# Attention values computed query by query: probabilities stationary, attention split by token and then turned

## The reference, cut to what matters

```python
def _L0_attn_ref(x, W_attn, b_attn, W_proj, b_proj):      # x: (2, 2048, 256), 16 heads of 16
    qkv = x @ W_attn + b_attn
    q, k, v = split(qkv)                                   # heads: (b, 16, t, 16)
    scores = einsum('bhtd,bhsd->bhts', q, k) * 0.25
    mask = (j <= i) & (j >= i - 64)                        # local, causal
    attn = softmax(where(mask, scores, -inf))
    out = einsum('bhts,bhsd->bhtd', attn, v)               # the step that the change rewrites
    return out.reshape(b, t, c) @ W_proj + b_proj

x = layernorm(x + attention(x))
# then a routed FFN: argmax router over 8 experts, W1[e] (256 x 1024), gelu, shared Wo
x = layernorm(x + ffn(x))
```

## Time and profile before

| what | value |
|---|---|
| median of 3 runs | 600.46 us (595.09 to 601.87) |
| the profiled execution, its own time | 598.72 us |
| span of its trace | 597.0 us |
| mean granted clock of TensorE | 0.957 |
| PE / DVE / ACT / POOL busy | 518.8 / 430.5 / 364.2 / 333.5 us |
| first instruction stretch, attention loop, tables, FFN | about 0 to 44, 44 to 352, 352 to 365, 365 to 597 us |

### The profile page before, as it was taken

One profiled execution on the slowest core, in us unless ns is written; L12 is line 12 of the kernel. 1 busy time (PEld: TensorE's weight loads), 2 busy tenths in 40 slices (PEclk: granted clock), 3 DMA queues, 4 the chain that ended last, 5 costly groups with the idle time before them and its releaser, 6 DMA issues. The chain is left out here.

```text
span 597.0 us, 29744 instructions
## 1 busy us (share of the span) xinstructions
PE 518.8 (87%) x11019; PEld 445.0 (75%) x11019; DVE 430.5 (72%) x1137; ACT 364.2 (61%) x832; POOL 333.5 (56%) x579
## 2 busy tenths in 40 slices
PE   4689896999999999989887716999999999999990
PEld 3577684877787777777775505999999999998870
DVE  4437784888788777877876665688888888886543
ACT  3436673787775757666674723766677676675450
POOL 7821442455553446444554541588888888886433
PEclk9869997999999999999999966999999999999996
DMA  9696987586757776566745102133322222221100
GB/s 202 152 213 175 244 237 201 157 189 182 200 164 210 172 202 178 164 183 187 191 140 152 38 27 68 52 100 97 94 83 73 66 81 74 74 73 49 31 9 7
DMA packets 94908, 77.46 MB, mean 130 GB/s; under 512 B 37030, under 2 KB 88367, under 8 KB 94770
## 3 DMA queue, kind: packets, MB, share of 16 engines
q1 hardware_dynamic: 91410, 67.12, 43.4%
q0 software_dynamic: 3264, 8.41, 4.0%
q10 hardware_dynamic: 96, 0.04, 0.0%
HBM read 43.63 MB, written 23.62 MB: 113 GB/s over the span
## 5 line engine op out<-in xcount | busy, mean ns | idle before, releaser
L1447 PE MATMUL ps<-v_even,w_hi 128*128 128x128 f16 (+1 forms) x1280 | 170.5, 215 | 1.7 <-issue 0.7
L1447 PE MATMUL ps<-v_even,w_lo 128*128 128x128 f16 (+1 forms) x640 | 132.1, 214 | 0.2
L853 ACT ACTIVATE probs<-ps,b1T 128x128 f32<-128x128 f32 (+1 forms) x320 | 87.3, 361 | 72.1 <-PE ps L1447 60.4
L1429 PE MATMUL ps<-wo_hi,ks 128*128 128x256 f16 x576 | 128.6, 273 | 1.0 <-DVE ks L1113 1.0
L1447 PEld LDWEIGHTS ps<-v_even,w_hi 128*128 x1280 | 120.8, 98 | 6.4 <-issue 3.1
L892 DVE TENSOR_REDUCE mx<-ps 128x4 bf16<-128x512 f32 x128 | 84.5, 683 | 18.9 <-PE ps L1219 18.0
L1429 PE MATMUL ps<-wo_lo,ks 128*128 128x256 f16 x288 | 78.5, 272 | 0.0
L1271 PE MATMUL ps<-probs,sel 128*32 128x64 f32 x2048 | 67.0, 220 | 6.4 <-issue 6.4
L745 ACT ACTIVATE probs<-ps 128x512 f32<-128x512 f32 x128 | 69.5, 617 | 2.7 <-PE ps L1245 2.6
L1113 DVE TENSOR_TENSOR ks<-probs,ks 128x512 f16<-128x512 f32 x72 | 55.1, 765 | 19.4 <-ACT ks L860 19.2
L1447 PEld LDWEIGHTS ps<-v_even,w_lo 128*128 x640 | 62.7, 98 | 6.2 <-issue 0.5
(11 more groups left out here) (232 smaller groups left out, 1360.1 us busy)
## 6 DMA issues: line engine op xcount, KB each, us to landing
qk_s<-qk_hi SPq DMA_DIRECT2D x64, 128.0 KB
w_in<-in_L_ffn_W_dram SPq DMA_DIRECT2D x32, 256.0 KB, 4.5
v_odd<-slots SPq DMA_DIRECT2D x64, 128.0 KB, 2.1
qs<-qk_s SPq DMA_DIRECT2D x16, 384.0 KB, 4.4
ks<-qk_s SPq DMA_DIRECT2D x16, 384.0 KB, 5.3
v_even<-v_odd SPq DMA_DIRECT2D x63, 96.0 KB, 4.0
ks<-qk_s SPq DMA_DIRECT2D x32, 144.0 KB, 4.0
qk_s<-qk_lo SPq DMA_DIRECT2D x32, 128.0 KB
```

Of the source, the lines that this page charges most:

```text
L853: last = nc.scalar.activation(g[1 - p][:, ic, n * width:(n + 1) * width], ps_h[1 - p][:, half, col + n * width:col + (n + 1) * width], ACT ...
L1429: ins = mm(ps_y[p], h[p][hs][:, ic, :], wo[ws][:, ic, :], start=n == 0, stop=n == 3 * IC - 1)
L1447: up_ins = mm(ps_h[1 - p][:, half, col + m * width:col + (m + 1) * width], weights(ws, owners[m], k, ic), sT[1 - p][ss][:, k, at], start=k ...
```

## The change

The value matmuls are turned round. For each head and each block of 64 queries the probabilities (128 keys x 64 queries) are the stationary operand and v of that head moves, 16 columns and a 17th that holds W_UP = 64 and so gives the denominator. The result (`ps_num`) has queries on the partitions, 16 heads x 17 columns. `sel`, `spread`, `less` and their set-up are gone. DVE takes the reciprocal of 128 x 16 denominators and multiplies at once (`att`, tokens x 256 channels), both now ahead of bn_stats. POOL splits `att` as before. PE then turns the two f16 parts with four transposes, which stand behind all four pieces of queries and keys and wait for POOL's `al_done`; ACT copies the result (`attT`, 512 f16 columns) where it copied rdenT. The projection of old moves from behind the x transposes to directly behind scores(0). values(0) and values(1) now take a half of the heads each; values(0) stands behind the x transposes and waits for three of the four exponentials, values(1) behind scores(3).

```diff
-    VW = 3 * HD
+    VW = HD + 1
...
-        v_odd = [sb(f"v_odd{k}", [P, PAIRS, VW], f32) for k in range(VRING)]
-        v_even = [sb(f"v_even{k}", [P, PAIRS, VW], f32) for k in range(VRING)]
+        v_odd = [sb(f"v_odd{k}", [P, HEADS, VW], f32) for k in range(VRING)]
+        v_even = [sb(f"v_even{k}", [P, HEADS, VW], f32) for k in range(VRING)]
...
+        rden = sb("rden", [P, HEADS], f32)
+        att = sb("att", [P, C], f32)
+        att_part = [sb(f"att_{s}", [P, C], f16) for s in ("hi", "lo")]
+        attT = sb("attT", [P, 2, CC, P], f16)
...
+        ps_num = ps[:, 6, 0:HEADS * VW].rearrange("p (h w) -> p h w", h=HEADS)
+        ps_attT = ps[:, 7, 0:C].bitcast(f16).rearrange("p (s k t) -> p s k t", s=2, k=CC)
...
+            link(nc.gpsimd.tensor_copy(ident_h[:, :], ident[:, :]))
...
-            link(nc.gpsimd.memset(sel[:, :, :], DEN))
...
-            link(nc.gpsimd.memset(spread[:, :, :], 0.0))
...
             for k in range(VRING):
-                nc.gpsimd.memset(v_odd[k][:, :, :], 0.0)
+                nc.gpsimd.memset(v_odd[k][:, :, :], W_UP)
...
                     pool.wait_ge(att_done, n + 1)
-                    wait(pool, proj_done, n)
-                    nc.gpsimd.tensor_copy(attT[0][:, :, :], att[:, :, :]).then_inc(ah_done, 1)
+                    wait(pool, attT_done, n)
+                    nc.gpsimd.tensor_copy(att_part[0][:, :], att[:, :]).then_inc(ah_done, 1)
                     pool.wait_ge(ah_done, n + 1)
-                    nc.gpsimd.tensor_tensor(attT[1][:, :, :], att[:, :, :], attT[0][:, :, :], ALU.subtract)\
+                    nc.gpsimd.tensor_tensor(att_part[1][:, :], att[:, :], att_part[0][:, :], ALU.subtract)\
                         .then_inc(al_done, 1)
...
-                    act.wait_ge(rdenT_done, n + 1)
-                    wait(act, att_done, n)
-                    nc.scalar.activation(rdenT[:, :, :], ps_rden, ACT.Copy).then_inc(rdenT_out, 1)
+                    act.wait_ge(attT_done, n + 1)
+                    wait(act, proj_done, n)
+                    nc.scalar.activation(attT[:, :, :, :], ps_attT, ACT.Copy).then_inc(attT_out, 1)
...
-                    dve.wait_ge(pv_done, 4 * done + 4)
-                    wait(dve, rdenT_done, done)
-                    wait(dve, rdenp_done, done)
-                    nc.vector.reciprocal(rden[:, :], ps_den).then_inc(rden_done, 1)
+                    dve.wait_ge(pv_done, CC * (done + 1))
+                    wait(dve, att_done, done)
+                    nc.vector.reciprocal(rden[:, :], ps_num[:, :, HD]).then_inc(rden_done, 1)
                     dve.wait_ge(rden_done, done + 1)
-                    nc.vector.tensor_copy(rden_hi[:, :], rden[:, :]).then_inc(rdenh_done, 1)
-                    dve.wait_ge(rdenh_done, done + 1)
-                    nc.vector.scalar_tensor_tensor(rden_parts[:, :], rden_hi[:, :], less[:, :], rden[:, :],
-                                                   ALU.mult, ALU.add).then_inc(rdenp_done, 1)
+                    wait(dve, al_done, done)
+                    nc.vector.tensor_tensor(att[:, :].rearrange("p (h d) -> p h d", d=HD), ps_num[:, :, 0:HD],
+                                            rden[:, :].unsqueeze(2).broadcast_to([P, HEADS, HD]), ALU.mult)\
+                        .then_inc(att_done, 1)
...
-                if a_tile(done):
-                    dve.wait_ge(rdenT_out, done + 1)
-                    wait(dve, al_done, done)
-                    nc.vector.tensor_tensor(att[:, :, :], ps_num, rdenT[:, :, :], ALU.mult).then_inc(att_done, 1)
...
                     if step == 3:
-                        wait(pe, rdenT_out, done + 1)
+                        wait(pe, attT_out, done + 1)
...
-                    pe.wait_ge(exp_done, 4 * done + step + 1)
-                    if step == 0:
+                    pe.wait_ge(exp_done, 4 * done + CC + c + 1)
+                    if c == 0:
...
-                    for e in range(2):
-                        for i in range(STRIPS):
-                            mm(ps_num[32 * i:32 * i + 32, u, :], v[:, STRIPS * c + i, HD * e:HD * e + 2 * HD],
-                               probs[:, u, i, e, :], start=step + e == 0, stop=e == 1,
-                               tile_position=(0, 32 * i), skip_group_check=True)
-                        for i in range(STRIPS):
-                            last = mm(ps_den[32 * i:32 * i + 32, :], sel[:, 2 * u + e, :], probs[:, u, i, e, :],
-                                      start=False, stop=step == UNITS_T - 1 and e == 1,
-                                      tile_position=(0, 32 * i), skip_group_check=True)
+                    for i in range(STRIPS):
+                        for e in range(2):
+                            head = 2 * (STRIPS * c + i) + e
+                            for b in range(2):
+                                v = (v_odd if b else v_even)[done % VRING]
+                                last = mm(ps_num[BLK * b:BLK * b + BLK, head, :], probs[:, 2 * c + b, i, e, :], v[:, head, :],
+                                          start=True, stop=True, tile_position=(0, BLK * b), skip_group_check=True)
                     last.then_inc(pv_done, 1)

                 scores(0)
-                values(0)
-                values(1)
+                if a_tile(old):
+                    pe.wait_ge(attT_out, old + 1)
...
+                    product(ps_proj, [(attT[:, 0, c, :], attT[:, 1, c, :]) for c in range(CC)],
+                            [(wp[0][:, c, :], wp[1][:, c, :]) for c in range(CC)]).then_inc(proj_done, 1)
                 scores(1)
...
-                if a_tile(old):
-                    pe.wait_ge(al_done, old + 1)
...
+                values(0)
                 scores(2)
                 scores(3)
-                values(2)
-                values(3)
+                values(1)
...
-                queries_keys((0, 1, 2))
+                queries_keys(range(2 * CC))
                 if a_tile(done):
-                    pe.wait_ge(rdenp_done, done + 1)
+                    pe.wait_ge(al_done, done + 1)
                     pe.wait_ge(exp_done, 4 * done + 4)
-                    for u in range(UNITS_T):
-                        for i in range(STRIPS):
-                            r = slice(32 * i, 32 * i + 32)
-                            last = mm(ps_rden[r, u, :], spread[:, u, r], rden_parts[:, :], start=True, stop=True,
-                                      tile_position=(0, 32 * i), skip_group_check=True)
-                    last.then_inc(rdenT_done, 1)
-                queries_keys((3,))
+                    wait(pe, attT_out, done)
+                    for part in range(2):
+                        for k in range(CC):
+                            last = nc.tensor.transpose(ps_attT[:, part, k, :], att_part[part][:, k * P:(k + 1) * P], ident_h[:, :])
+                    last.then_inc(attT_done, 1)
```

More of the change, by code:

```diff
@@ L120, in attention_then_routed_ffn @@
         ident_b = sb("ident_b", [P, P], bf16)
+        ident_h = sb("ident_h", [P, P], f16)
         shut = sb("shut", [1, P], bf16)
-        sel = sb("sel", [P, 2 * UNITS_T, 32], f32)
-        spread = sb("spread", [P, UNITS_T, P], f16)
         before = sb("before", [P, P], bf16)
@@ L453, in _ @@
                     sp.wait_ge(v_out, m + 1)
-                    wait(sp, pv_done, 4 * (m - VRING) + 4)
+                    wait(sp, pv_done, CC * (m - VRING + 1))
                     sp.dma_start(v_even[m % VRING][BLK:P, :, :], v_odd[m % VRING][0:BLK, :, :])\
@@ L457, in _ @@
                     if a_tile(m + 1):
-                        wait(sp, pv_done, 4 * (m + 1 - VRING) + 4)
+                        wait(sp, pv_done, CC * (m + 2 - VRING))
                         sp.dma_start(v_even[(m + 1) % VRING][0:BLK, :, :], v_odd[m % VRING][BLK:P, :, :])\
@@ L593, in _ @@
             link(nc.gpsimd.memset(fill[:, C:ROW], float(NO_TOKEN)))
-            link(nc.gpsimd.memset(sel[:, :, :], DEN))
-            link(nc.gpsimd.affine_select(out=sel[:, :, :], in_=sel[:, :, :], compare_op=ALU.is_ge, fill=0.0,
-                                         base=0, pattern=[[-4, 2 * UNITS_T], [1, 32]], channel_multiplier=0))
-            link(nc.gpsimd.affine_select(out=sel[:, :, :], in_=sel[:, :, :], compare_op=ALU.is_ge, fill=0.0,
-                                         base=3, pattern=[[4, 2 * UNITS_T], [-1, 32]], channel_multiplier=0))
-            link(nc.gpsimd.memset(spread[:, :, :], 0.0))
-            for u in range(UNITS_T):
-                for part in range(2):
-                    link(nc.gpsimd.affine_select(
-                        out=spread[:, u, :].rearrange("p (i e d) -> p i e d", e=2, d=HD),
-                        in_=spread[:, u, :].rearrange("p (i e d) -> p i e d", e=2, d=HD),
-                        compare_op=ALU.not_equal, fill=W_DOWN * DEN, base=-8 * u - part,
-                        pattern=[[-32, STRIPS], [-4, 2], [0, HD]], channel_multiplier=1))
             for k in range(VRING):
```

(18 more changed lines are left out.)

36 lines of the change are left out of this document (11 added, 25 removed).

## The result

| what | before | after |
|---|---|---|
| median | 601.16 us (4 runs, 595.09 to 604.44) | 631.36 us (4 runs, 630.91 to 635.29) |
| ratio to before | | 1.056, 95% interval 1.048 to 1.063 |
| the profiled execution and its span | 598.72, 597.0 us | 635.29, 633.6 us |
| mean granted clock of TensorE | 0.957 | 0.916 |
| PE / DVE / ACT / POOL busy | 518.8 / 430.5 / 364.2 / 333.5 | 523.3 / 397.6 / 370.0 / 325.9 us |

A forecast was written before the change was run, and what follows sets the result against it. PE bound the kernel before; after, PE would wait about 1.8 us a turn for POOL's split. Turn 5.96 + 4.2 + 0.1 stall = 10.25 us; +4.5, +17.8, +3.5, +0.4 on 598.7 gave 625 us, range 610 to 645.

The forecast's parts named there:

- T to R: Start of the new att transposes on PE to start of DVE's reciprocal: PE's stream, 5.96 us a turn.
- R to T: Start of DVE's reciprocal to start of PE's transposes: reciprocal and att 0.62, POOL's chain 3.56, 0.04; 4.2 us.
- First reciprocal: Start of the first DVE reciprocal: left at 48.2 us, with POOL's smaller set-up counted as 0.
- First six intervals: First six reciprocal intervals: 5 x 10.25 + 16.8 - 1 = 67.0 us against 62.5 before, +4.5.
- Middle 21: The 21 middle reciprocal intervals: 10.25 us each, 215.3 us against 197.5 before, +17.8.
- DVE "close": DVE's path from T to the reciprocal, R at T + 6.3 taken whole; PE's 5.96 was kept instead.
- Last four: Last four intervals, without queries and keys or x transposes: 3 x 9.9 + 8.5 = 38.2 us against 34.7, +3.5.
- Behind the last reciprocal: After the loop's last reciprocal: a turn and copy at PE's lower clock more, +0.4 us.
- Rival 3: PE's standstill lowers its granted clock; 656 us if a turn lost 1 us by it; 4%.
- Rival 1: PE stays the bound, the split done under 2.4 us of cover: turn 8.9 us, about 583 us; 6%.
- Value matmuls: 64 records a tile in place of 128, 0.93 us per 32, 1.86 a tile; no PE time gained.
- Rival 2: Value matmuls' weight loads run in sequence: 3.7 us a tile, 57 us more, 682 us; 7%.

The follow-up runs named there:

- Experiments 1 and 2: Changed kernel with POOL's split ahead of its statistics: 587.94 us; extra POOL copy before the split: 654.54 us in the changed kernel, ratio 1.0007 in the kernel before.
- experiment 7: DVE's w_lo moved to just ahead of qk_lo, behind a wait for the split: 616.44 us in the changed kernel, 581.59 us in the kernel of experiment 5.
- experiment 3: Changed kernel plus 24 unused 128x128x128 f16 matmuls a turn in PE's wait, ahead of the transposes: 624.76 us, ratio 1.033.
- experiment 1: Changed kernel with POOL's split of att ahead of its statistics (less_mean to shift_by): 587.94 us; the two faster executions 582.99 and 583.97.
- experiment 5: Kernel of experiment 1 with the residual's bias on POOL also moved behind shift_by: 578.41 us, ratio 0.958.
- experiment 6: Unused matmuls added a turn: to experiment 5's kernel 13 large, 578.90 us, or 75 small, 599.84; 8 large, 576.98; to the changed kernel 100 small, 645.02.

## Why the prediction was right, and where its numbers were off

**The mechanism and the turn.** The sum has T to R 5.96 and R to T 4.2. In the profile after, T to R is 5.95 in 16 of 31 turns, R to T 4.15 to 4.32 in nearly all, and ordinary turns are 10.1 and 10.3 us. What it said would show, shows: transposes that wait for att_lo (1.8 us in the turn above, within 1.5 to 2.2), POOL without idle from shift_by to the split, 32 value records in 0.95 us, PE's busy time hardly changed, fewer issue waits. Experiments 1 and 2 show that POOL's order causes it: taking its statistics out of the way gives 48 us back, and 0.39 us more on POOL costs 0.35 a turn after the change and nothing before it. R to T of 4.2 was right partly by luck. I took 3.56 us of it from the earlier trace rows as one piece, and that piece already held less_mean at 0.65, which was not its own length but w_lo's hold on it (experiment 7). I used the durations 0.19 and 0.66 of shift_by as bounds without asking why they differ; 0.4 us a turn hung on it.

**The Trainium skill**, in SBUF — State Buffer, section "SBUF: two separate sides", says that VectorE and GpSimd share a pair of ports which a VectorE instruction with two SBUF inputs locks for its whole length against a GpSimd instruction that reads SBUF. Experiment 7 agrees: w_lo has two SBUF inputs, and 0.37 to 0.48 us of POOL's time vanish with it.

**The sum against the profiled execution** (span 633.6 us; the forecast of 625 is a span of 623.3). First reciprocal: counted as unchanged at 48.2, came at 45.6, -2.6; POOL's smaller set-up was costed at 0. How much of the 2.6 is the set-up stays open: no run takes it alone, and the first reciprocal comes anywhere from 44.1 to 47.7 in the kernels that share the new set-up. First six intervals: 67.0 forecast, 64.9 measured; the long one, kept at 16.8 less 1, was 12.1, but another rose to 13.7, by a standstill in "issue" of 3.1 us. Middle 21: 215.3 forecast, 221.6 measured, +6.3. The 13.2 at the half clock is 3.0 of it, and the 12.6 with its 2.2 us of "issue" is 2.4 longer than its neighbours, about what the sum had left for stalls (0.1 a turn, 2.1). Three turns are 0.4 longer for another reason: DVE has a piece of FFN weights to split there, and comes 0.4 us late to the reciprocal; the prediction had DVE "close", and there it decides. In such a turn, DVE (PE's stream is the same as in others to 0.01 us):

```profile
127.59 0.68 DVE L1017 SCALAR_TENSOR_TENSOR wo_lo<-w_lo,wo_hi 128x512 f16<-128x512 f32 x1
128.19 1.28 DVE L868 TENSOR_REDUCE mx<-ps 128x4 bf16<-128x512 f32 x2
...
131.32 0.25 DVE L923 RECIPROCAL rden<-ps 128x16 f32<-128x16 f32 x1
```

Last four: 38.2 forecast, 46.9 measured, +8.7, the largest miss, and the half clock again. Behind the last reciprocal +0.5, where +0.4 was forecast.

**Rival 3, the clock**, had 4% as a case by itself at 1 us a turn. It wasn't that: it came on top, at some 7 us in all (experiment 3). The step that failed was judging the clock by PE's busy share over a stretch. The changed kernel's loop has 81%, more than the 77% of the stretch at 1.00, and yet it lost clock. Three falls (93.3, 147.9 and 199.1) came 3 to 4 us after the start of standstills of 2.1 to 2.3 us; but other standstills of 2.0 and 2.1 passed without a fall, and the small-matmul kernels have falls at standstills of 1.2 and 1.3 us. Which standstill brings a fall stays open.

**Rival 1**, 583 us if the split were done under cover, was the right account of what held the kernel: experiment 1 gives 588 (583.5 with the faster executions) and experiment 5 gives 578. Its condition ("without POOL's statistics ahead") was named, and the diff didn't meet it. I wrongly gave the 8.9 us turn 0.2 us of stalls: it is 8.6.

**Value matmuls.** "Fewer records, but no PE time gained" is right for the busy time. But the gain of the new form lies elsewhere: 252 records a turn became 176, and most of the issue waits went, 17.2 us over the loop before, 2.8 in experiment 5. The pair of experiment 6 puts 19 us on such a difference; my sum had 0.4 us a turn for it (0.1 of stall left in place of 0.5), 12 us. In the kernel as changed 9.6 us of issue waits are left, two of which made long turns, while one inside the wait for att_lo is all but free: in the turn shown, PE loses 1.1 us to "issue" from 262.2 and waits only 0.48 us for att_lo afterwards. **Rival 2** (weight loads in sequence) is refuted: 0.95 us for 32 records, not 1.9.

## What to carry over

When a result that used to be needed a turn later becomes needed in the same turn, walk the whole queue of the engine that makes it: here 1.6 us of one-column statistics, an indirect DMA and a bias stood ahead of the split, free before and 1.8 us a turn after, and moving two blocks turned +6% into -4%. Count instructions beside busy time: of two kernels with the same PE time, the one with 62 records more a turn was 19 us slower. Where one instruction has two durations, find out what runs beside it before taking either as its cost.

## What the runs showed of the hardware

- The granted clock of TensorE fell to 0.50 (1.2 GHz) 3 to 4 us after the start of some standstills of 2.1 to 2.3 us, and stayed at 1.00 after nearly all of 1.6 to 1.8. 24 unused matmuls in the wait kept it up for most of the loop, and made the kernel 6.6 us faster.
- PE's issue waits, 0.2 to 4.8 us each, are more with many PE records: 12.6 to 20.3 us over the loop at 251 to 276 records a turn (four traces), 0 to 9.6 at 176 to 200. They come at distances close to multiples of 125 matmul records.
- A POOL instruction that starts while DVE's w_lo runs ends only behind it (less_mean and shift_by 0.05 us behind): one of 0.19 us takes 0.56 to 0.67, one of 0.40 takes 0.86. The other way round, w_lo takes 1.13 us for 0.69 where the bias on POOL started first.
- f32 weights of 64 columns in the two halves of the array: 0.029 us per record (32 in 0.95 with the switch of shapes), against 0.12 for 128 columns. Half the columns would be 0.06 one after the other, so loads of the two halves do overlap.
